# Two layers of cross-attention and feed-forward on one core: the first attention's gate moves from TensorE to VectorE, its output scaling and context normalisation change engines, and the scattered operands get separate slots

## The reference, cut to what matters

```python
qn = layer_norm(query, ln_q_g, ln_q_b)          # query is layernorm(x)
kn = vn = layer_norm(ctx, ln_kv_g, ln_kv_b)
q, k, v = qn @ Wq + bq, kn @ Wk + bk, vn @ Wv + bv
out = softmax(q k^T / sqrt(8)) v  @ Wo + bo      # per head
gate = sigmoid(qn @ Wg)                          # one number per token
x = x + layer_norm(gate * out, ln_o_g, ln_o_b)
```

## Time and profile before

| | us |
|---|---|
| median of 3 runs (960.68 to 964.42) | 961.96 |
| the profiled execution's own time | 960.1 |
| its span, first to last instruction | 958.2 |
| first attention, about | 0 to 268 |
| first feed-forward | 268 to 623 |
| second attention | 619 to 848 |
| second feed-forward | 848 to 958 |

### The profile page before, as it was taken

How to read it: one execution, slowest core, us unless ns; L and a number is a source line. 1 busy time by engine, 2 the same in 40 slices (tenths; PEclk the granted TensorE clock), 3 DMA queues, 4 the chain that set the end, 5 groups by cost and what they waited for, 6 DMA issues and landing times.

```text
span 958.2 us, 32911 instructions
## 1 busy us (share of the span) xinstructions
PE 917.0 (96%) x12349; PEld 709.6 (74%) x12349; DVE 694.0 (72%) x2046; ACT 753.3 (79%) x1350; POOL 358.9 (37%) x543
## 2 busy tenths in 40 slices
PE   5999999999989999999999999989999999999998
PEld 3677777777657888888887888756777777768886
DVE  7778888787786766666666766466766676589985
ACT  7577777778778888888888888667777777678986
POOL 5889999997521000000000000154444544021110
PEclk9999999999999999999999999999999999999999
DMA  6333322211000000000000000122222221100111
GB/s 215 92 99 93 103 68 85 73 46 41 19 1 1 1 0 0 0 0 0 0 0 0 0 0 1 50 77 74 68 63 68 69 69 52 31 2 34 44 44 56
DMA packets 46691, 41.71 MB, mean 44 GB/s; under 512 B 24416, under 2 KB 32864, under 8 KB 46560
## 3 DMA queue, kind: packets, MB, share of 16 engines
q1 hardware_dynamic: 45456, 37.12, 12.6%
q10 hardware_dynamic: 1104, 2.77, 0.8%
HBM read 16.79 MB, written 4.19 MB: 22 GB/s over the span
## 4 chain that ended last, share of the span: by engine, by line
PE 77%; DVE 11%; DMA 4%; issue 3%; ACT 2%; SPq 2%; ACTq 0%; POOL 0%; DVEq 0%; POOLq 0%
PE ps_w L1134 15%; PE ps_w L1133 15%; PE ps_w L560 5%; PE ps_w L563 5%; DMA qk_sets<-qk_t 4%; DVE top L890 4%; PE ps_av L616 3%; PE ps_w L546 3%; PE ps_mid L672 3%; PE ps_av L650 3%; PE ps_y L659 2%; DVE stats L919 2%; PE ps_turn L578 2%; SPq L518 2%; PE g_ps_out L1133 2%
## 5 line engine op out<-in xcount | busy, mean ns | idle before, releaser
L890 DVE TENSOR_REDUCE top<-ps_w 128x16 f32<-128x1024 f32 x128 | 156.5, 1223 | 107.6 <-PE ps_w L560 107.2
L1133 PE MATMUL ps_w<-g_h_lo,w_hi 128*128 128x512 f32 x512 | 206.0, 402 | 1.8 <-DVE g_h_lo L1388 1.7
L1134 PE MATMUL ps_w<-g_h_hi,w_hi 128*128 128x512 f32 x512 | 202.2, 395 | 0.0
L1388 DVE TENSOR_TENSOR g_h_lo<-g_h,g_h_hi 128x512 fp32r<-128x512 f32 x192 | 132.6, 690 | 86.3 <-ACT g_h_hi L1326 82.4
L133 POOL TENSOR_TENSOR front_rstd<-front_spread,minus_half 128x4 f32<-128x4 f32 x33 | 36.3, 1099 | 388.4 <-DVE front_spread L126 388.4
L715 ACT ACTIVATE prob_t<-ps_w 128x1024 f32<-128x1024 f32 x128 | 130.7, 1021 | 19.3 <-PE ps_w L563 19.1
L560 PE MATMUL ps_w<-qk_sets,qk_t 32*64 32x256 f32 x2048 | 141.8, 387 | 3.0 <-DMA qk_sets<-qk_t 2.8
L1326 ACT ACTIVATE g_h_hi<-g_h 128x512 fp32r<-128x512 f32 x192 | 121.3, 632 | 18.5 <-DVE g_h L1398 14.4
L563 PE MATMUL ps_w<-qk_sets,qk_t 32*64 32x256 f32 x2048 | 133.3, 375 | 0.0
L1133 PEld LDWEIGHTS ps_w<-g_h_lo,w_hi 128*128 128x128 f32 x512 | 96.2, 188 | 25.2 <-DVE g_h_lo L1388 3.5
L1134 PEld LDWEIGHTS ps_w<-g_h_hi,w_hi 128*128 128x128 f32 x512 | 96.4, 188 | 21.3
(11 more groups left out here) (164 smaller groups left out, 2037.5 us busy)
## 6 DMA issues: line engine op xcount, KB each, us to landing
qk_sets<-qk_t SPq DMA_DIRECT2D x254, 64.0 KB, 1.9
ctx_in<-in_ctx SPq DMA_DIRECT2D x32, 128.0 KB, 3.1
ctx_in<-in_ctx_t SPq DMA_DIRECT2D x32, 128.0 KB, 2.4
out_x<-x_res SPq DMA_DIRECT2D x15, 256.0 KB, 2.0
x_res<-in_x SPq DMA_DIRECT2D x14, 256.0 KB, 3.3
shift<-pieces SPq DMA_DIRECT2D x128, 16.0 KB, 2.3
w_raw<-in_ff_weights SPq DMA_DIRECT2D x8, 256.0 KB, 3.1
w_raw<-in_ff_weights ACTq DMA_DIRECT2D x1, 768.0 KB, 8.9
```

The source lines that it names most:

```text
L890: nc.vector.tensor_reduce(out=top[:, i % 2, half, :], in_=bank_pair(half).rearrange("p (a q) -> p a q", q=SEQ), op=ALU.max, axis=AX.X).the ...
L1133: nc.tensor.matmul(out, w_hi, x_lo, start=first and w_lo is None, stop=False)
L1134: return nc.tensor.matmul(out, w_hi, x_hi, start=False, stop=last)
L1388: nc.vector.tensor_tensor(h_lo[level][:, o, :], h[:, o % 2, :], h_hi[level][:, o, :].bitcast(F32), ALU.subtract).then_inc(lo_ready[level], 1)
```

## The change

- The gate: L668 and its waits are gone. At the end of its step j VectorE forms the gate of unit j+3 with two `scalar_tensor_tensor` that multiply the normalised x by a row `gate_row` and accumulate the row sum. The opening makes `gate_row` (one copy, one product on TensorE, one copy out of PSUM). POOL waits for the gate of the unit before last before it overwrites `normed`.
- The context: ScalarE normalises the context of unit j+4 (from unit 3 on) in two `Identity` activations with scale and bias by pointer, right after `take_qk`; POOL makes the bias, minus mean times reciprocal deviation, in two instructions on one column, after L853. POOL keeps the two instructions on x.
- The output rows: VectorE's L994 is gone. POOL does `(y - mean) * rstd` in two instructions with two pointers, then one product with `ln_o_g` over 256 columns, then the addition to x, each behind a wait on the one before.
- VectorE's order: `spread` and `top_middle` before `take_stats`, `top_low` after it, and `take_moments` after `top_low`.
- `qk_sets` has 5 slots for Q and 3 for K. A scatter waits for the shifted scores of unit j-3 and the plain scores of unit j-1 instead, in both attentions; in each partition it writes two runs of 1024 bytes. The clearing in the opening covers the same number of elements, the second time in two instructions instead of one.

```diff
@@ Opening and clearing @@
+GATE_ROW = slice(2 * P, 3 * P)
+Q_SLOTS, K_SLOTS = 5, 3
+FIRST_OPERANDS = slice(3, 7)
+def q_slot(i):
+    return (i + 3) % Q_SLOTS
+def k_slot(i):
+    return Q_SLOTS + i % K_SLOTS
...
+    nc.tensor.matmul(op.ps[:, GATE_ROW], op.wide[:, 3, :], t.ident[:, :], start=True, stop=True).then_inc(op.bias_done, 1)
...
+    nc.vector.tensor_copy(op.wide[:, 3, :], t.gate_col[:, :].to_broadcast([P, P]))
@@ scatter @@
-                queue.dma_start(qk_sets[m:P:SETS, s, m, :, :], qk_t[m:P:SETS, i % QKT, :, :]).then_inc(qk_landed[s], 16)
+                q, k = q_slot(i), k_slot(i)
+                queue.dma_start(qk_sets[m:P:SETS, q:k + 1:k - q, m, :], qk_t[m:P:SETS, i % QKT, :, :]).then_inc(qk_landed[s], 16)
@@ tensor @@
-                if gated:
-                    wait(pe, gate_exp_ready, upto(i - 1))
...
+                    if gated:
+                        wait(pe, ctx_normed, i + 1 - EARLY_UNITS)
...
-                    if gated:
-                        for k in range(UNIT_TILES):
-                            last = nc.tensor.matmul(ps_mid[:, UNIT + k:UNIT + k + 1], turned[:, i % TURNED, 0, k * P:(k + 1) * P],
-                                                    t.gate_col[:, :], start=True, stop=True)
-                        last.then_inc(gate_done, 1)
@@ scalar, after take_qk(j + 2) @@
+                i = j + 4
+                if gated and on(i) and i >= EARLY_UNITS:
+                    act.wait_ge(ctx_bias_ready, i + 1 - EARLY_UNITS)
+                    wait(act, in_t_done, i - 1)
+                    wait(act, normed_ready, EARLY_UNITS)
+                    for k in range(UNIT_TILES):
+                        last = nc.scalar.activation(normed[:, i % 2, 1, k, :], ctx_in[:, i % CTX, k, :], ACT.Identity,
+                                                    scale=rstd[:, i % UNROLL, 1, k:k + 1], bias=ctx_bias[:, i % UNROLL, k:k + 1])
+                    last.then_inc(ctx_normed, 1)
@@ gpsimd @@
-                    for n in range(NORMS):
-                        for k in range(UNIT_TILES):
-                            src = ctx_in[:, i % CTX, k, :] if n else t.x[:, span(i * UNIT_TILES + k, P)]
-                            last = nc.gpsimd.tensor_scalar(normed[:, i % 2, n, k, :], src, moments[:, s, n, k, 0:1],
-                                                           rstd[:, s, n, k:k + 1], ALU.subtract, ALU.mult)
+                    if gated:
+                        wait(pool, gate_done, i - 1)
+                    for k in range(UNIT_TILES):
+                        last = nc.gpsimd.tensor_scalar(normed[:, i % 2, 0, k, :], t.x[:, span(i * UNIT_TILES + k, P)], moments[:, s, 0, k, 0:1],
+                                                       rstd[:, s, 0, k:k + 1], ALU.subtract, ALU.mult)
...
+                    if gated and i >= EARLY_UNITS:
+                        pool.wait_ge(rstd_ready, i + 1)
+                        for k in range(UNIT_TILES):
+                            last = nc.gpsimd.tensor_scalar(ctx_bias[:, s, k:k + 1], moments[:, s, 1, k, 0:1], rstd[:, s, 1, k:k + 1], -1.0,
+                                                           ALU.mult, ALU.mult)
+                        last.then_inc(ctx_bias_ready, 1)
...
-                    pool.wait_ge(y_gain_ready, i + 1)
+                    wait(pool, x_done, i - 1)
                     for k in range(UNIT_TILES):
-                        last = nc.gpsimd.tensor_scalar(y_gain[:, i % 2, k, :], y_gain[:, i % 2, k, :], rstd[:, (i + CLOSING) % UNROLL, 2, k:k + 1], 0.0,
-                                                       ALU.mult, ALU.add)
+                        last = nc.gpsimd.tensor_scalar(y_gain[:, i % 2, k, :], y[:, i % UNROLL, k, :], y_moments[:, i % UNROLL, k, 0:1],
+                                                       rstd[:, (i + CLOSING) % UNROLL, 2, k:k + 1], ALU.subtract, ALU.mult)
                     last.then_inc(y_scaled, 1)
                     pool.wait_ge(y_scaled, i + 1)
+                    nc.gpsimd.tensor_tensor(y_gain[:, i % 2, :, :], y_gain[:, i % 2, :, :],
+                                            t.ln_o_g[:, :].unsqueeze(1).to_broadcast([P, UNIT_TILES, P]), ALU.mult).then_inc(y_gain_ready, 1)
+                    pool.wait_ge(y_gain_ready, i + 1)
@@ vector, end of the step @@
+                i = j + 3
+                if gated and on(i):
+                    dve.wait_ge(normed_ready, i + 1)
+                    wait(dve, gate_exp_ready, i + 1 - UNROLL)
+                    wait(dve, gate_done, i)
+                    for k in range(UNIT_TILES):
+                        last = nc.vector.scalar_tensor_tensor(out=gate_terms[:, k, :], in0=normed[:, i % 2, 0, k, :], scalar=1.0, in1=t.gate_row[:, :],
+                                                              op0=ALU.mult, op1=ALU.mult, accum_out=gate[:, i % UNROLL, k:k + 1])
+                    last.then_inc(gate_done, 1)
@@ sync @@
-                    wait(sp, shifted_done, 2 * (i - 3))
+                    wait(sp, shifted_done, 2 * (i + 1 - Q_SLOTS))
+                    wait(sp, scores_done, 2 * (i + 1 - K_SLOTS))
```

More of the change, by code:

```diff
@@ L191, in sem @@
             return outer.enter_context(nc.semaphore(f"open_{part}"))
-        self.wide = scratch[:, 0:3, :]
+        self.wide = scratch[:, 0:4, :]
         self.ps = ps
@@ L292, in clear_operands @@
 def clear_operands(nc, t, op, slots):
-    wide = t.qk_sets[:, slots, :, :, :].rearrange("p s m n u -> p (s m) (n u)")
-    nc.scalar.activation(wide, t.blank[:, :].unsqueeze(1).to_broadcast([P, FIRST_SLOTS * SETS, 512]), ACT.Copy).then_inc(op.slots_cleared, 1)
+    for part in slots:
+        wide = t.qk_sets[:, part, :, :].rearrange("p s m u -> p (s m u)").rearrange("p (a n) -> p a n", n=512)
+        last = nc.scalar.activation(wide, t.blank[:, :].unsqueeze(1).to_broadcast([P, (part.stop - part.start) * SETS * UNIT // 512, 512]), ACT.Copy)
+    last.then_inc(op.slots_cleared, 1)
 def clear_values(nc, t, op, slots):
@@ L452, in attention @@
             gate_exp = sb("gate_exp", [P, T])
+            gate = sb("gate", [P, UNROLL, UNIT_TILES])
+            gate_terms = sb("gate_terms", [P, UNIT_TILES, P])
+            ctx_bias = sb("ctx_bias", [P, UNROLL, UNIT_TILES])
             gate_sq = sb("gate_sq", [P, T])
@@ L498, in attention @@
         if gated:
+            ctx_bias_ready = sem("ctx_bias_ready")
+            ctx_normed = sem("ctx_normed")
+            gate_row_ready = sem("gate_row_ready")
             gate_done = sem("gate_done")
@@ L789, in step @@
                         act.wait_ge(gate_done, i + 1)
-                        nc.scalar.activation(gate_exp[:, span(i, UNIT_TILES)], ps_mid[:, UNIT:UNIT + UNIT_TILES], ACT.Exp,
+                        nc.scalar.activation(gate_exp[:, span(i, UNIT_TILES)], gate[:, i % UNROLL, :], ACT.Exp,
                                              scale=-1.0, bias=t.gate_nb[:, 0:1]).then_inc(gate_exp_ready, 1)
@@ L843, in step @@
                     if gated:
+                        wait(pool, ctx_normed, i - 3 - EARLY_UNITS)
+                    if gated:
                         nc.gpsimd.tensor_scalar(spread[:, s, 0, :], moments[:, s, 0, :, 1], 1.0 + EPS, EPS * EPS, ALU.mult, ALU.add)
@@ L967, in step @@
                     dve.wait_ge(y_chain, 2 * i + 1)
+                    wait(dve, y_scaled, i + 1 - UNROLL)
                     for k in range(UNIT_TILES):
@@ L972, in step @@
                     top_rest(j)
+                if gated and on(i):
+                    dve.wait_ge(y_chain, 2 * i + 2)
+                    dve.wait_ge(gate_sq_ready, i + 1)
+                    wait(dve, rstd_ready, i + CLOSING - UNROLL + 1)
+                    nc.vector.scalar_tensor_tensor(out=spread[:, (i + CLOSING) % UNROLL, 2, :], in0=gate_sq[:, span(i, UNIT_TILES)], scalar=EPS,
+                                                   in1=y_moments[:, i % UNROLL, :, 1], op0=ALU.mult, op1=ALU.add).then_inc(y_spread_ready, 1)
+                if gated and on(j):
+                    top_middle(j)
                 i = j + 5
@@ L983, in step @@
                 if on(j):
-                    top_middle(j)
-                i = j - 5
-                if gated and on(i):
-                    dve.wait_ge(y_chain, 2 * i + 2)
-                    dve.wait_ge(gate_sq_ready, i + 1)
-                    wait(dve, rstd_ready, i + CLOSING - UNROLL + 1)
-                    nc.vector.scalar_tensor_tensor(out=spread[:, (i + CLOSING) % UNROLL, 2, :], in0=gate_sq[:, span(i, UNIT_TILES)], scalar=EPS,
-                                                   in1=y_moments[:, i % UNROLL, :, 1], op0=ALU.mult, op1=ALU.add).then_inc(y_spread_ready, 1)
-                    wait(dve, x_done, i - 1)
-                    for k in range(UNIT_TILES):
-                        last = nc.vector.scalar_tensor_tensor(out=y_gain[:, i % 2, k, :], in0=y[:, i % UNROLL, k, :],
-                                                              scalar=y_moments[:, i % UNROLL, k, 0:1],
```

(9 more changed lines are left out.)

24 lines of the change are left out of this document (14 added, 10 removed).

## The result

Over all runs the changed kernel took 968.36 us in the median (967.05 to 970.39, 7 runs), the kernel before, on the same chips, 961.96 us (955.35 to 964.42): **1.0078 times the time before, 95% interval 1.0048 to 1.0108.** It is slower by more than the 0.5% named above, and just outside the range. The changed kernel's profiled execution took 968.36 us with a span of 964.6; the one before had 960.1 and 958.2.

The account below looks back on a forecast made before the run. POOL's 8.0 us round was to bound the first attention. +4.6 there, -2.3 after it and -5 for the scatter gave -2.7 us: 957.4 from the profiled 960.1, plus 1.9 to the median, 959.3 us; range 951 to 968.

Parts of the forecast that it names:

- The bound: First attention: POOL's round becomes 8.0 us, against 6.6 for the rest, and a late POOL holds up ScalarE and TensorE.
- over 10: First attention: ScalarE would idle over 10 us in all ahead of its `Identity`, waiting for POOL's column bias.
- the 941.5 us case: Rival, first attention: new output rows cost like the old ones, POOL's round 7.15 us, time 941.5 us; chance 0.06.
- The row sums: VectorE, end of each step: two row sums of the gate, priced at 0.34 us each, outside the ring.
- ScalarE's `Identity`: ScalarE, first attention: two `Identity` on 128 columns a round, priced at 0.28 us each, 0.56 together.
- The slack and the tail: First attention: 3.4 us of slack before ScalarE follows POOL; after step 27 lighter POOL rounds give -2.3 us.
- 21 rounds of 8.0 us: First attention, steps 5 to 26: POOL's rounds put step 26 8.0 us late, +4.6 us at step 27's end after slack.
- The rival with its 8.4 us round: First attention: contention lengthens POOL's round to 8.4 us, 21 rounds cost +8.4 us, time 967.7 us; chance 0.18.
- the scatter, -5 us: Second attention: the scatter, issued 0.5 to 0.9 us sooner, removes most of PE's 8.4 us idle; -5 us (0 to -8).
- a rival for "no gain": Second attention: the scatter's shorter runs eat its lead, so no gain there, time 964.3 us; chance 0.14.

Follow-up runs that it names:

- experiment 3: The changed kernel with only the gate put back on TensorE; 965.51 us, 1.0071 of the kernel before.
- experiment 13: The changed kernel with the gate back on TensorE, plus two unread VectorE row sums in each of 32 steps; 970.02 us.
- experiment 6: The changed kernel with the scatter's old wait, eight slots kept; 966.94 us, 1.0081 of the kernel before.
- experiment 7: The kernel before with only the eight slots, their layout and the scatter's earlier release; 959.72 us, 0.9998 of the kernel before.
- experiment 8: The kernel before with only the eight slots and their layout, scatter's old wait kept; 959.78 us, 1.0013 of the kernel before.
- experiment 10: The changed kernel with the output rows back on VectorE and the scatter's old wait; 948.0 us, 0.9901 of the kernel before.
- Experiment 2: The changed kernel with the output rows back on VectorE and the gate back on TensorE; 950.3 us, 0.9914 of the kernel before.
- experiment 9: The changed kernel with the context load issued behind the scatter, second attention only; 968.65 us, 1.0089 of the kernel before.
- experiment 14: The changed kernel with TensorE's two gate products added back, unread, beside VectorE's row sums; 970.44 us.
- experiment 1: The changed kernel with the output rows back on VectorE, gate left there; 946.55 us, 0.9894 of the kernel before.
- experiment 4: The changed kernel without GpSimd's product of the output rows with `ln_o_g`; 951.16 us, 0.9924 of the kernel before.
- experiment 11: The changed kernel with the output rows back on VectorE, new scatter wait, measured once more; 947.21 us, 0.9874 of the kernel before.
- experiment 12: The changed kernel with the gate back on TensorE, plus one unread VectorE row sum in step 8; 969.03 us.

## Why the prediction was wrong

**Right.** The bound: POOL's round sets the first attention, and the chain, ScalarE's waits (27.2 us, "over 10" was said) and TensorE's waits behind them are as described. The new output rows cost 1.57 us a pair like other work with two pointers, not like L867, so the 941.5 us case was rightly small. The row sums: 0.33 us each, as priced from the earlier trace rows, and 0.08 for reading the sum. ScalarE's `Identity` took 0.88 us a pair instead of 0.56, beside its wait and so for nothing. The slack and the tail: from step 26 to the feed-forward the changed kernel gained 5.0 us, forecast 3.4 + 2.3.

**The step that failed first: the term "21 rounds of 8.0 us".** Measured 8.245, 5.1 us too little, and with that the end of step 27. Of the 21 rounds fifteen take 8.10 us in the mean. From the start of one instruction to the start of the next, these have the column bias at 0.46 us, as priced (0.45); the power with the wait behind it grew from 1.31 to 1.48 us, 0.17 where 0.1 was priced; the output rows grew from 0.80 to 1.71, 0.91 where 0.86 was priced, the excess in the rounds where they lie beside the gate's row sums. Together that is the 0.1 us over 8.0. The other six, at 8.49 to 8.83, mean 8.60, are those beside a weight split: 6 x 0.5 = 3.0 us, the larger half. The prediction had this price in hand (0.72 against 1.15) and argued that the old round already holds 0.2 us of it. Those 0.2 us are another stretch, that of the context's instruction beside VectorE's old `y_gain` (0.98 instead of 0.79 us), and they went with the 1.77 us that the sum took off. The split's 0.4 us stood in two old rounds of 21. The same split, in two rounds of the kernel before (timeline):

```profile
85.22 1.11 DVE L259 TENSOR_TENSOR w_lo<-w_raw,w_hi 128x512 fp32r<-128x512 f32 x1
85.77 1.15 POOL L867 TENSOR_SCALAR y_gain<-y_gain,rstd 128x128 f32<-128x128 f32 x2
...
114.36 1.34 POOL L853 TENSOR_TENSOR rstd<-spread,minus_half 128x6 f32<-128x6 f32 x1
115.08 0.66 DVE L259 TENSOR_TENSOR w_lo<-w_raw,w_hi 128x512 fp32r<-128x512 f32 x1
115.68 0.73 POOL L861 TENSOR_TENSOR x_res<-x_res,rows 128x256 f32<-128x256 f32 x1
```

In steps 6 and 8 it met the pair L867 and stretched it; from step 10 on it fell beside the power, which stays at 1.34 us, and it ended 0.06 to 0.15 us after L861 had begun, and the round stayed at 7.51. In the changed kernel GpSimd's order stands otherwise against VectorE's, and all six splits meet an instruction with pointers: once the column bias, once the normed x, four times the output rows, as in the round shown above:

```profile
69.57 1.09 POOL L885 TENSOR_SCALAR ctx_bias<-moments,rstd 128x1 f32<-128x1 f32 x2
...
82.73 2.26 POOL L853 TENSOR_SCALAR normed<-x_res,moments,rstd 128x128 f32<-128x128 f32 x2
```

Whether a split costs 0.5 us or nothing is thus a matter of what starts beside it, and the prediction didn't ask. The rival with its 8.4 us round thus had the right mechanism, but for six rounds and not for all; the row sums themselves add only the 0.1 us that experiments 3 and 13 show. The Trainium skill, GPSIMD Engine Reference, Specifications, has the contention as a matter of VectorE's instructions with two SBUF inputs; the runs agree for the split (2.09 against 1.57 us) and show that it was 0.5 us for the one form and about 0.1 us a round for the other.

**The step that failed second: the scatter, -5 us.** The waits for the scatter did go (8.4 to 0), as said, but experiments 6 to 8 and 10 put their worth at 0, with bounds of about 1.8 us. The prediction read the earlier trace rows as "PE stood idle 8.4 us in 16 places, 0.5 us in the mean". That sum counts the weight loads' waits beside the products' own: the products stood still for 2.8 us in seven places, so the trace that the term was taken from held no 5 us of such waits. And the prediction took a wait that ended last as time to be had, whole. It had a rival for "no gain", at 0.14, though for another reason (shorter runs), which experiment 8 does not bear out: the layout alone costs nothing measurable, and the transfers still land in 1.9 us. Why not even the 2.8 us come back is not settled. TensorE's pauses without a recorded cause, of 0.9 us and more, don't settle it: they stand in traces with the early release (the changed kernel) and with the old wait (the kernel before, experiment 8), and only experiments 6 and 10 are without.

**Not in the sum at all:** 1.9 us outside the span, which no view of the kernel before could show.

These make the difference: 5.1 + 3.0 + 1.9, with 1.2 - 0.2 us of small ones, is the 11.0 us.

## What to carry to other kernels

When work is moved to an engine that the stage's windows show without a pause, its whole cost lands in every round, and so does every stretch that another engine causes in it; for each contending instruction, ask which of the engine's instructions will start beside it in the new order, and in how many rounds. Ask of each part of a bundle what it is worth alone: here the output rows' move cost 18 to 19 us and hid a gain of 1.0 to 1.3% that the other parts had made. Experiment 2, which has the gate back as well, keeps 0.9%; with the scatter worth nothing, that leaves the context's move to ScalarE and VectorE's new order, which no run took apart. A wait that ends last is not yet time to be had: undo it alone before counting on it, and look first whether the sum counts one wait on two rows.

## What the runs showed of the hardware

**A dropped clock in the opening.** The first attention of experiment 9 has the changed kernel's code, yet its step 5 comes at 63.13 us instead of 59.37. The windows show why (columns as above; the third from the end is the granted clock), first of the changed kernel, then of experiment 9:

```profile
28.00:32.00 4.00, 3.95 (x47) 2.55 (x41) 2.51 (x8) 2.70 (x8) 3.31 (x6) 1.00 0.18 53
32.00:36.00 4.00, 4.00 (x33) 2.29 (x32) 3.63 (x15) 2.52 (x8) 1.64 (x4) 1.00 0.46 133
```

```profile
28.00:32.00 4.00, 4.00 (x27) 2.82 (x27) 1.79 (x7) 0.92 (x4) 1.85 (x4) 0.50 0.22 70
32.00:36.00 4.00, 3.95 (x28) 2.46 (x28) 1.49 (x3) 1.76 (x5) 1.56 (x2) 0.76 0.38 107
```

With 0.89 between 24 and 28 us, TensorE ran at 1.2 GHz, half of its speed, for (0.11 + 0.50 + 0.24) x 4 / 0.5 = 6.8 us, and step 5 came 3.8 us later. Around the start of the drop TensorE's work is thin, 2.23 us busy of 4 between 24 and 28 us, but so it is in the changed kernel, whose clock stayed at 1.00. Experiments 2, 3, 13 and 14 had clocks of 0.72 to 0.86 between 24 and 32 us and step 5 at 62.4 to 63.0; experiments 1, 4, 10 and 11 had 0.80 to 0.84 between 20 and 24 us and step 5 at 59.85 to 60.97. Without any drop, step 5 came at 59.37 and 60.75 with the gate on VectorE (changed kernel, experiment 6) and at 61.70 with it on TensorE (experiment 12). So both the clock and the gate's place move step 5, and differences of 3 us between these kernels' times need not come from their edits.

**Two engines' instructions stretch each other,** and mostly the one that starts second takes the longer. A VectorE subtraction of 512 columns in SBUF and a GpSimd addition of two tensors of 256 columns, twice in experiment 4 (timelines of the two engines):

```profile
110.52 0.67 DVE L270 TENSOR_TENSOR w_lo<-w_raw,w_hi 128x512 fp32r<-128x512 f32 x1
110.66 1.11 POOL L904 TENSOR_TENSOR x_res<-y_gain,x_res 128x256 f32<-128x256 f32 x1
...
125.66 0.72 POOL L904 TENSOR_TENSOR x_res<-y_gain,x_res 128x256 f32<-128x256 f32 x1
125.82 1.11 DVE L270 TENSOR_TENSOR w_lo<-w_raw,w_hi 128x512 fp32r<-128x512 f32 x1
```

Where the subtraction is first, the addition ends 0.58 us after it; where the addition is first, it stays at 0.72 us and the subtraction grows from 0.67 to 1.11. The same holds with pointers: GpSimd instructions that start with or within the subtraction grow, by up to 0.7 us and the less the later they start (even the column bias, two columns in all: 1.09 us against 0.50). Two exceptions stand in the traces: GpSimd's power, running when the subtraction starts, leaves it at 0.66 to 0.68 us and stays at 1.34 itself, and an instruction with two pointers that is 0.3 us or more under way leaves it at 0.67. Why, no run shows.

**The own time and the span** differ by about 1.8 us in one group of kernels and by about 3.5 in the other, in every run. Comparing spans alone would have missed it.
